# Seven groups of full-precision products on TensorE, and the third image fold and spread moved on GpSimd, in a fused patch-embedding, attention and mixture-of-experts kernel

## The reference

```
pooled = x.reshape(B, 12, 14, 16, 14, 16).sum(axis=(3, 5))        # patches of 16 x 16
h = concat(einsum('bcij,ce->bije', pooled, channel_weights), txt)  # 196 + 32 = 228 tokens of 192
h = h + attention(layernorm(h))      # 12 heads of 16, rotary, causal, a sink column in the softmax
z = layernorm(h)
probs = softmax(z @ gate_w.T); top_p, top_i = top_k(probs, 2)      # 8 experts
pos = running count of each expert over all tokens; keep = pos < cap
buf[expert * cap + pos] = z                                        # dispatch
y = buf + (silu(g) * u) @ w2,  g, u = split(rmsnorm(2 * buf) * norm_w @ w13)
h = h + sum over the token's two experts of weight * y
```

## Time and profile before

| | |
|---|---|
| time, median of 3 runs | 2894.42 us (2891.46 to 2895.87) |
| the profiled execution's own time | 2893.81 us |
| its span in the trace | 2892.0 us |
| mean granted TensorE clock | 0.982 |
| busy: TensorE, VectorE, ScalarE, GpSimd | 95%, 71%, 59%, 70% |

### The profile page before, as it was taken

One profiled execution on the slowest core, in us unless ns is written; L12 is line 12 of the kernel. 1 busy time (PEld: TensorE's weight loads), 2 busy tenths in 40 slices (PEclk: granted clock), 3 DMA queues, 4 the chain that ended last, 5 costly groups with the idle time before them and its releaser, 6 DMA issues. The chain is left out here.

```text
span 2892.0 us, 65150 instructions
## 1 busy us (share of the span) xinstructions
PE 2744.5 (95%) x21264; PEld 2447.2 (85%) x21264; DVE 2066.9 (71%) x5722; ACT 1700.2 (59%) x4074; POOL 2020.2 (70%) x2070
## 2 busy tenths in 40 slices
PE   2899999999999999999999959999999999999998
PEld 1788888888888888888888848999999999999997
DVE  3577777777777777777777736767676767676766
ACT  1466666666666666666666635656565656555655
POOL 3578888888888888888888724655566656565655
PEclk9899999999999999999999969999999999999999
DMA  6455555444444434444444023233333333424242
GB/s 190 146 179 178 175 169 172 156 124 124 124 123 122 115 113 114 116 124 123 124 124 122 26 57 64 45 66 48 66 47 67 50 66 53 69 43 67 41 70 43
DMA packets 206150, 292.44 MB, mean 101 GB/s; under 512 B 95800, under 2 KB 167819, under 8 KB 206018
## 3 DMA queue, kind: packets, MB, share of 16 engines
q1 hardware_dynamic: 82786, 241.38, 28.5%
q0 software_dynamic: 122880, 47.00, 11.6%
q10 hardware_dynamic: 352, 2.41, 0.3%
HBM read 201.70 MB, written 93.90 MB: 102 GB/s over the span
## 5 line engine op out<-in xcount | busy, mean ns | idle before, releaser
L1505 POOL DMA_INDIRECT out<-arena,who x320 | 595.6, 1861 | 294.1 <-DVE who L1384 180.8
L694 POOL TENSOR_TENSOR arena<-arena 112x896 f32<-112x896 f32 x192 | 402.9, 2099 | 12.8 <-DMA arena<-in_x 12.8
L1478 PE MATMUL bank<-w_dn,hid 128*114 128x192 f32 x3840 | 401.9, 264 | 0.0
L1478 PEld LDWEIGHTS bank<-w_dn,hid 128*114 128x114 f32 x3840 | 390.3, 180 | 0.0
L576 DVE TENSOR_REDUCE top<-bank 114x2 f32<-114x456 f32 (+1 forms) x576 | 349.8, 622 | 46.9 <-PE bank L939 34.7
L1451 ACT ACTIVATE arena<-bank 128x456 f32<-128x456 f32 x320 | 176.4, 551 | 346.0 <-PE bank L1442 335.4
L1296 POOL DMA_INDIRECT moe_rows<-row,slot x256 | 294.0, 1149 | 102.9 <-issue 84.5
L553 ACT ACTIVATE pieces<-bank 64x456 fp32r<-64x456 f32 x384 | 208.1, 542 | 134.0 <-PE bank L915 131.7
L1455 DVE TENSOR_TENSOR arena<-bank,arena 128x456 f32<-128x456 f32 x320 | 201.4, 629 | 96.4 <-ACT arena L1451 83.3
L1438 PE MATMUL bank<-pieces 128*128 128x456 f32 x640 | 241.2, 377 | 20.9 <-DVE arena L1455 13.9
L734 POOL TENSOR_TENSOR qk<-rot_c,qk 114x384 fp32r<-114x384 f32 x256 | 253.2, 1011 | 8.7 <-ACT qk L755 4.3
(11 more groups left out here) (167 smaller groups left out, 6994.9 us busy)
## 6 DMA issues: line engine op xcount, KB each, us to landing
arena<-in_x SPq DMA_DIRECT2D x63, 2352.0 KB, 12.0
arena<-moe_rows SPq DMA_DIRECT2D x82, 363.4 KB
moe_rows<-filler SPq DMA_DIRECT2D x20, 1453.5 KB
out<-h SPq DMA_DIRECT2D x64, 171.0 KB
out<-arena,who POOLq DMA_INDIRECT x320, 5.0
arena<-in_w_t SPq DMA_DIRECT2D x9, 512.0 KB
arena<-in_w_t SPq DMA_DIRECT2D x18, 256.0 KB
moe_rows<-row,slot POOLq DMA_INDIRECT x256, 7.2
```

Of the source, the lines that this page charges most:

```text
L694: nc.gpsimd.tensor_tensor(xin[at.par][:, g, 0:mid], xin[at.par][:, g, 0:mid], xin[at.par][:, g, mid:XF], ALU.add).then_inc(x_folded, 1)
L1478: ins = nc.tensor.matmul(dst, hid2[:, j, h_part, at], w_dn2[e_par][:, j, w_part, :], start=(j == 0 and s % 2 == 0 and part == 0), stop=(j ...
L1505: nc.gpsimd.indirect_dma_start(out=out[:, :], out_offset=bass.IndirectOffsetOnAxis(ap=who[par][:, s:s + 1], axis=0), in_=ys[par][:, s, :], ...
```

## The change

On TensorE, S3 goes ahead of `turn_xn`, `gate_logits` goes ahead of C4 and S5, and `rank` goes ahead of S7 and C6. `turn_xn` then stands with `attend` and `make_qk`, `gate_logits` with `turn_xf` and `make_qk`, and `rank` with `attend`. On VectorE, `choose` goes ahead of the maxima 4 and 5, and the third `pool_image` goes from ahead of `assign` to behind `place_k` 1. On GpSimd, the third `fold_image` goes from between the two rotations to behind the remainders. `scatter_rows` now issues two of the four scatters per call; the spreads of groups 0 and 1 come ahead of the first two scatters, and that of group 2 between the second and the third. The semaphore `x_spread` counts each spread, and `sum_channels` still waits for all three.

```diff
@@ pool_image / sum_channels
-                wait(dve, x_spread, at.b - 1)
+                wait(dve, x_spread, NG * (at.b - 1))
...
-            pe.wait_ge(x_spread, n)
+            pe.wait_ge(x_spread, NG * n)
@@ spread_patches
-        def spread_patches(pool, at):
+        def spread_patches(pool, at, groups):
             wait(pool, h_summed, at.b)
-            for g in range(NG):
+            for g in groups:
                 pool.wait_ge(x_pooled, NG * at.b + g + 1)
-                ins = nc.gpsimd.tensor_tensor(...)
-            ins.then_inc(x_spread, 1)
+                nc.gpsimd.tensor_tensor(...).then_inc(x_spread, 1)
@@ step_tensor
-            ring("S1 C1 S2 C2")
+            ring("S1 C1 S2 C2 S3")
             if a:
                 turn_xn(pe, a)
-            ring("S3")
             if t:
                 attend(pe, t, 0)
...
-            ring("C4 S5")
             if z:
                 gate_logits(pe, z)
-            ring("C5 S6")
+            ring("C4 S5 C5 S6")
             if t:
                 attend(pe, t, 1)
-            ring("S7 C6")
             if z:
                 rank(pe, z)
-            ring("S8 C7 C8")
+            ring("S7 C6 S8 C7 C8")
@@ step_vector
-            maxima("4 5")
             if z:
                 choose(dve, z)
-            maxima("6")
-            if p:
-                pool_image(dve, p, 2)
+            maxima("4 5 6")
             if z:
                 assign(dve, z)
...
             if a:
                 place_k(dve, a, 1)
+            if p:
+                pool_image(dve, p, 2)
             if m:
                 split_shift(dve, m)
@@ pass1_gpsimd
                 if a:
                     add_rotation(pool, a, 0)
-                if p:
-                    fold_image(pool, p, 2)
                 if a:
                     add_rotation(pool, a, 1)
                     low_parts(pool, a, 0)
                     low_parts(pool, a, 1)
                 if p:
-                    spread_patches(pool, p)
+                    fold_image(pool, p, 2)
+                    spread_patches(pool, p, (0, 1))
                 if gone:
                     scatter_waits(pool, gone, fill)
+                    scatter_rows(pool, gone, 0)
+                if p:
+                    spread_patches(pool, p, (2,))
+                if gone:
+                    scatter_rows(pool, gone, 1)
@@ scatter_rows
-            for t in range(2):
-                for k in range(TOPK):
-                    nc.gpsimd.indirect_dma_start(...).then_inc(scattered[at.par], 16)
+            for k in range(TOPK):
+                nc.gpsimd.indirect_dma_start(...).then_inc(scattered[at.par], 16)
```

More of the change, by code:

```diff
@@ L695, in fold_image @@
                                     ALU.add).then_inc(x_folded, 1)
-        def spread_patches(pool, at):
+        def spread_patches(pool, at, groups):
             wait(pool, h_summed, at.b)
-            for g in range(NG):
+            for g in groups:
                 pool.wait_ge(x_pooled, NG * at.b + g + 1)
-                ins = nc.gpsimd.tensor_tensor(spread[:, g, :].rearrange("p (i j) -> p i j", j=SIDE),
+                nc.gpsimd.tensor_tensor(spread[:, g, :].rearrange("p (i j) -> p i j", j=SIDE),
                                               pooled[at.par][:, g, :].unsqueeze(1).to_broadcast([XP, SIDE, SIDE]),
-                                              patch[:, :].unsqueeze(2).to_broadcast([XP, SIDE, SIDE]), ALU.mult)
-            ins.then_inc(x_spread, 1)
+                                              patch[:, :].unsqueeze(2).to_broadcast([XP, SIDE, SIDE]), ALU.mult).then_inc(x_spread, 1)
         def inverse_std(pool, at, norm):
@@ L1265, in one @@
                 if p:
-                    spread_patches(pool, p)
+                    fold_image(pool, p, 2)
+                    spread_patches(pool, p, (0, 1))
                 if gone:
                     scatter_waits(pool, gone, fill)
+                    scatter_rows(pool, gone, 0)
[3 more added lines that the diff above has]
+                    scatter_rows(pool, gone, 1)
                 if known is not None and known >= B:
                     scatter_waits(pool, z, fill)
+                    scatter_rows(pool, z, 0)
+                    scatter_rows(pool, z, 1)
             for i in range(PEEL):
@@ L1288, in scatter_waits, with scatter_rows @@
                 pool.wait_ge(filled[z.par], 16 * (FILLS // 2))
[L1289 to L1293, removed]
-            for t in range(2):
-                for k in range(TOPK):
[L1296 to L1300, removed]
+            pool.wait_ge(row_whole, z.b + 1)
+            hold(pool, routed, z.b + 1, held)
+        def scatter_rows(pool, at, t):
+            for k in range(TOPK):
+                nc.gpsimd.indirect_dma_start(
+                    out=moe_rows[0:SLOTS, :],
+                    out_offset=bass.IndirectOffsetOnAxis(ap=slot[at.par][:, 2 * t + k:2 * t + k + 1], axis=0),
+                    in_=row[at.par][:, t, :], in_offset=None, bounds_check=SLOTS - 1, oob_is_err=False,
+                ).then_inc(scattered[at.par], 16)
         rows_n = moe_rows.rearrange("(n p s) w -> n p s w", p=TT, s=SUB)
```

## The result

The changed kernel takes 2960.68 us (median of 4 runs, 2951.37 to 2974.55), beside 2895.14 us of the kernel before (4 runs on the same chip): 1.0227 times as long, 95% interval 1.0204 to 1.025. The profiled execution of the changed kernel took 2962.9 us (span 2961.1), 69.1 more than that of before.

What follows compares the result with a forecast made beforehand. TensorE was taken to bound pass 1 at 25.01 us a step. From the profiled 2893.8 us, adding 51 (loop) and 6 (filling) less 1 (TensorE) gave 2949 us; own range 2932 to 2970, full range 2924 to 2978.

Steps and rivals of the forecast that it cites:

- The loop: From one `sum_channels` to the next, through GpSimd's late third spread: 25.89 us a step against 25.01, 51 us over 58 periods.
- the gap from a scatter to a computing instruction: On GpSimd, ahead of the third spread: no row shows it; between 0 and 0.30 us, taken as 0.15.
- putting the transposes of xn behind S3: On TensorE: delays by some 0.5 us the copy the first `make_qk` waits for; cost taken as 0, at most 0.15.
- Rival 2: Same loop but cheaper, by no gap or a 0.3 shorter path to `make_qk`: 2905 to 2930 us; chance 0.09.
- the remainders as 3.95 us: On GpSimd, remainders up to the next instruction: 3.99 us, of which some 0.04 was waiting for ScalarE, leaving 3.95.
- The filling steps: The 15 steps with filling: later scatter landings hold ScalarE's second norm, 0.4 us a step within 0 to 1.7; 6 us.
- rival 3: Moved image load holds the scatters' rows beyond the room: 2970 us in filling steps, 2990 if others too; chance 0.08.
- the 1 us of room: At ScalarE's second norm, ahead of the second `make_qk`: a landing 1 us later counted as free.
- TensorE's 0.3 us: On TensorE: fewer changes of product kind (0.21) and `rank` meeting no wait (0.1) save some 0.3 us, lost in the wait.
- Rival 1: The third spread is in time and TensorE's joined groups pay about 22 us: 2872 us, faster; chance 0.05.
- the third pooling's new place: On VectorE, in the 1.15 us hole ahead of `split_shift`: the 1.08 us pooling costs nothing if the fold is done.
- what I said would show me wrong: `sum_channels` without a wait, spread following the scatter by far over 0.3 us, or ScalarE's scattered-row wait the longest new one.

Runs made afterwards that it cites:

- E5: The changed kernel with one scatter ahead of the third spread and the other three behind it: 2948.18 us, 1.0179 times the kernel before.
- E6: The changed kernel with all four scatters ahead of the third spread: 3236.63 us, 1.1172 times the kernel before.
- E7: The changed kernel with score block S3 put back behind `turn_xn`, other groups still joined: 2953.22 us, 1.0198 times the kernel before.
- E3: The kernel before with only GpSimd's new order and the third pooling's new place; TensorE's order and `choose` as before: 3027.62 us, 1.0433 times the kernel before.
- E8: The changed kernel with all 16 fills of the row buffer issued in the first step instead of one a step: 3139.17 us, a single run.
- E1: The changed kernel with GpSimd's order as before and the third pooling behind maximum 6; TensorE's groups and early `choose` stay: 2919.15 us, 1.0066 times the kernel before.
- E4: The changed kernel with the third fold back between the rotations, two scatters still ahead of the third spread: 2938.52 us, 1.0142 times the kernel before.
- E10: The changed kernel with GpSimd's order as before and the third pooling ahead of maximum 6; all three TensorE groups joined: 2897.6 us, 1.0004 times the kernel before.
- E2: The changed kernel with all three spreads ahead of all four scatters, fold still behind the remainders: 2955.24 us, 1.0185 times the kernel before.
- E9: The changed kernel with GpSimd's order as before, the third pooling ahead of maximum 6 and S3 behind `turn_xn`: 2894.36 us, 0.999 times the kernel before.

## Why the prediction was right, and where it was not

**The loop is what was forecast.** The step without filling is 25.81 us, forecast 25.89. Its parts, from the two timelines above: `sum_channels` to the second `make_qk` 858.05 - 846.40 = 11.65 (11.57 forecast); from there to the second sums 2.65 (2.58 and 0.08); sums and remainders 839.91 - 834.93 = 4.98 (5.06); fold 2.05 (2.06); two spreads and setup 1.21 (1.20); two scatters and the gap behind 845.81 - 843.17 = 2.64 (2.62 and 0.15); third spread and release 0.59 (0.57). Over 58 steps, 58 x (25.81 - 24.95) = 50 us, against 51. E5 and E6 show that this loop sets the step, by the scatters in it. I had no row for the gap from a scatter to a computing instruction and took 0.15; it is 0.02.

**Two misses in the first part cancelled.** I took 0, at most 0.15, for putting the transposes of xn behind S3. It costs 0.25 up to the first `make_qk`, and undoing it gives 0.28 a step (E7). That the path to the second `make_qk` still measured what I had read from before comes from the other side: from the turn of y to S0 it takes 848.76 - 848.44 = 0.32 in the changed kernel; before, 837.83 - 837.26 = 0.57, as the timeline shows:

```profile
837.26 0.63 PE L1015 MATMUL bank<-ident,yn 114*97 114x114 f32 x4
837.83 0.46 PE L964 MATMUL bank<-pieces 128*115 128x456 f32 x1
```

Before, `normalize` ended just as these transposes began; the stop gives it the time. Rival 2 had named this shortening ("0.3 shorter once TensorE has stood still"); I had not set it against the copy of xn. That the sum came out is luck here.

**A third term was right for a reason that I did not give.** I took the remainders as 3.95 us, with no wait for ScalarE's rounding, though the sums ahead of them now start 0.45 earlier. E3 shows that with the choice in its old place this wait is 0.52 us a step (30 us in 58 steps), and that the stop behind it is then 0.3 us longer, with the clock falling behind most of them. The early choice removes it; I had reckoned the choice only for `rank`.

**The filling steps were under-sized.** I put their extra at 0.4 us a step, 6 us. They grew by 26.94 - 25.20 = 1.74, of which the loop gives 0.86: 0.88 a step, 13 us. This is inside my bounds of 0 and 1.7 (the load's 2.6 us less the 1 us of room give 1.6), and not "nearer the lower end". The mechanism was the one I gave (rival 3 in part): landings in the steps with filling take 9.8 us in the median instead of 7.5, and E8 removes the extra with the filling. The prediction read the Trainium skill ("DMA: Bandwidth & Descriptors", section "SWDGE vs HWDGE vs iDMA"), by which each DMA engine serves its queues in turn, to mean that other queues would not hold the scatters; these landings don't bear that reading out. The image load is issued 3.1 us ahead of `sum_channels`, 5.9 before (3.3 forecast). E1 and E4 speak for it: they differ in the third pooling's place, behind which the load is issued (5.9 and 2.1 us ahead), and in two scatters ahead of the third spread; the step without filling is the same (25.30 and 25.32), with filling 25.41 and 26.57. No run moved the load alone.

**"TensorE's 0.3 us" was wrong,** though it did not enter the sum, since it fell into the wait. The groups with the early choice gave 0.07 where VectorE's third pooling is arranged for them (E10) and cost 0.35 where it stands behind maximum 6 (E1). Rival 1, which rested on them with 22 us gained, would have been off even had the spread been in time: E2, E4 and E5, without the wait, still take 2938 to 2955 us. That the third pooling's new place "costs nothing" held, even without the stop (E5); in E4, where VectorE's small instructions take 0.51 us longer beside GpSimd's, `normalize` is 0.42 us late for TensorE.

**The sum**: 50 from the loop, 13 from the filling, 1.5 at the start and 4.2 behind step 63, together 69; forecast 51 + 6 - 1 = 56. The time, 2960.68, lies 12 us above 2949 and inside both ranges. Of what I said would show me wrong nothing appeared. Of the signs, the wait ahead of the second sums is 1.59, forecast 1.5, and the stop ahead of `sum_channels` 0.94, forecast about 1; the waits on landed rows grew more than I said (31.4 us in the steps with filling, before 24.0).

What stays open: why E10 gains from the three groups only a third of the 0.21 worked out from the change of kinds; what the step of E2 goes by (25.22, with no stop of more than 1.1 us behind step 20); and what share of the 4.2 us behind step 63 belongs to the change (E9 and E10, with no change there, have 9 and 4 more than before between step 63 and the end).

## What to carry to other kernels

When an instruction is moved past others in a queue, follow the loop that goes through its consumer around the step and back, with every instruction that it is now behind; here that sum came within 0.1 us of 25.8, two of its terms with some luck. Do not credit the rest of a change with what it would gain alone: an engine whose work is only reordered can lose more (0.35 us a step) to one late hand-over of another engine than it gains from the order (0.07). Before a wait is removed, look at what it covers; here the stop hid a `normalize` slowed beside GpSimd (E4), late landings and, at E5 and E2, a fall of the clock behind these, so that each partial repair gave back less than its term.

## What the runs showed of the hardware

- TensorE's granted clock. Behind a stop of 0.92 to 0.96 us in each step it stayed at 1.00 from 600 to 1600 us. With a stop of 1.20 to 1.25 us (E3) it fell in 26 of 36 steps, and the products behind took 3.1 to 3.9 us instead of 2.2; behind 3.8 us (E6) they took exactly twice as long in every step of that stretch, which is the 1.2 GHz level. The length of one stop does not decide alone: E3 has falls and no falls behind the same stop, and the changed kernel, in a step with filling, stood 1.65 us in front of `turn_xf` at a clock of 1.00. The price of a stop has a jump in it that no sum of durations shows.
- The gap between two scatters on GpSimd is 0.30 us, but a computing instruction follows a scatter by 0.02 and the next scatter needs 0.19 to 0.22 of setup.
- Two of VectorE's small instructions take longer while GpSimd works. The copy of the token numbers (L662, shown at E4) takes 0.16 us in the median of the kernel before; beside the scatter that runs from 856.84 to 857.98 it ends with it, after 0.53 us (also E4's median), and in the changed kernel it takes 0.55. The Trainium skill ("GPSIMD Engine Reference", section "1. Specifications") says that GpSimd shares its way to SBUF with VectorE, and that VectorE's instructions in a 2-port mode contend for it; by that rule the trace agrees, with 0.53 against 0.16 us, but whether this copy runs in such a mode no trace here says. E4 beside E5 shows what it can cost: 0.51 us in VectorE's chain, of which TensorE waits 0.42 in each step.

```profile
856.84 1.14 POOL L1296 DMA_INDIRECT moe_rows<-row,slot  x1 [0.19 <-issue]
```
